# Attention of an audio tower: padded projection weights, folded scale, softmax row sums from a ones column

## The reference, cut to what matters

```python
q = jnp.einsum('bqd,hdm->bqhm', x, W_Q) + b_Q          # k and v alike
scores = jnp.einsum('bqhm,bkhm->bhqk', q, k) / jnp.sqrt(jnp.asarray(D_HEAD, q.dtype))
scores = jnp.where(causal[None, None, :, :], scores, jnp.asarray(IGNORE, scores.dtype))
pattern = jax.nn.softmax(scores, axis=-1)
z = jnp.einsum('bhqk,bkhm->bqhm', pattern, v)
attn_out = jnp.einsum('bqhm,hmd->bqd', z, W_O) + b_O
```

## Time and profile before

| | us |
|---|---|
| median of 3 runs | 1911.6 (1901.9 to 1912.4) |
| span of the profiled execution | 1912.2 |
| PE busy | 1539.1 |
| VectorE busy | 1109.6 |
| ScalarE busy | 757.7 |
| GpSimd busy | 600.9 |

### The profile page before, as it was taken

How to read it: one execution, slowest core, us unless ns; L and a number is a source line. 1 busy time by engine, 2 the same in 40 slices (tenths; PEclk the granted TensorE clock), 3 DMA queues, 4 the chain that set the end, 5 groups by cost and what they waited for, 6 DMA issues and landing times.

```text
span 1912.2 us, 33119 instructions
## 1 busy us (share of the span) xinstructions
PE 1539.1 (80%) x10013; PEld 1020.7 (53%) x10014; DVE 1109.6 (58%) x2520; ACT 757.7 (40%) x1456; POOL 600.9 (31%) x502
## 2 busy tenths in 40 slices
PE   6975699998865899889657999898659999339997
PEld 4332476783333666763334666833336667327775
DVE  5986455568884555669864555598845555302221
ACT  2643344425542444425533444165324443002221
POOL 3732133305431333236322333064213331421111
PEclk6987799998986999979877999989869999659999
DMA  4200121210000221110001222100014332621110
GB/s 125 80 1 1 34 57 41 56 34 12 1 1 1 65 56 41 33 36 1 1 1 40 53 48 51 30 11 1 1 28 105 89 73 66 199 69 46 48 47 20
DMA packets 105852, 81.31 MB, mean 43 GB/s; under 512 B 57842, under 2 KB 96267, under 8 KB 105747
## 3 DMA queue, kind: packets, MB, share of 16 engines
q1 hardware_dynamic: 99988, 70.65, 14.6%
q0 software_dynamic: 5760, 9.36, 1.6%
HBM read 34.66 MB, written 18.38 MB: 28 GB/s over the span
## 4 chain that ended last, share of the span: by engine, by line
issue 40%; PE 35%; POOL 15%; DVE 5%; SPq 2%; DMA 2%; ACT 1%; POOLq 0%; DVEq 0%; ACTq 0%
POOL arena L794 10%; PE ps L1676 8%; PE ps L1618 6%; PE ps L1650 4%; PE ps L1662 3%; PE ps L1830 3%; PE ps L1625 2%; PE ps L1810 2%; PE ps L1811 2%; DVE arena L1212 2%; DVE smax L1203 2%; POOL slot_scratch L848 1%; PE ps L1818 1%; SPq L552 1%; PE ps L1831 1%
## 5 line engine op out<-in xcount | busy, mean ns | idle before, releaser
L1723 PE MATMUL ps<-arena,cwt 128*128 128x504 f16 (+2 forms) x1776 | 409.8, 392 | 85.3 <-DVE arena L1178 59.9
L1723 PEld LDWEIGHTS ps<-arena,cwt 128*128 128x128 f16 x1776 | 179.4, 105 | 305.9 <-DVE arena L1178 66.2
L794 POOL TENSOR_TENSOR arena<-arena 128x1008 f16<-128x1008 f32 (+2 forms) x112 | 255.6, 2292 | 196.6 <-DVE arena L1178 196.6
L1676 PE MATMUL ps<-arena 128*128 128x64 f32 (+2 forms) x2016 | 261.2, 270 | 22.9 <-DVE arena L1212 22.9
L1203 DVE TENSOR_REDUCE smax<-ps 128x1 f32<-128x128 f32 (+5 forms) x288 | 177.2, 615 | 172.1 <-PE ps L1653 172.1
L1676 PEld LDWEIGHTS ps<-arena 128*128 128x128 f32 (+2 forms) x2016 | 242.3, 189 | 44.2 <-issue 28.5
L1212 DVE COPY arena<-ps 128x512 f32<-128x512 f32 (+4 forms) x288 | 157.4, 546 | 83.7 <-PE ps L1662 83.6
L1181 DVE TENSOR_TENSOR arena<-arena 128x1008 f16<-128x1008 f32 (+2 forms) x88 | 200.3, 2276 | 3.0
L917 ACT ACTIVATE arena<-ps,nmax 128x128 f32<-128x128 f32 (+5 forms) x288 | 180.6, 627 | 53.5 <-DVE nmax L1204 50.7
L1178 DVE CAST arena<-arena 128x1008 f16<-128x1008 f32 (+4 forms) x200 | 176.9, 914 | 32.6 <-ACT arena L903 16.1
L1650 PE MATMUL ps<-arena 128*128 128x512 f16 (+6 forms) x780 | 163.7, 313 | 28.9 <-ACT arena L957 16.3
(11 more groups left out here) (249 smaller groups left out, 2181.1 us busy)
## 6 DMA issues: line engine op xcount, KB each, us to landing
arena<-arena SPq DMA_DIRECT2D x96, 187.5 KB, 2.9
arena<-arena SPq DMA_DIRECT2D x96, 93.8 KB, 2.5
slot_scratch<-empty_slot SPq DMA_DIRECT2D x1, 5775.0 KB, 18.6
arena<-in_L_ffn_w SPq DMA_DIRECT2D x8, 576.0 KB
arena<-in_L_ffn_w SPq DMA_DIRECT2D x8, 384.0 KB
arena<-slot_scratch SPq DMA_DIRECT2D x31, 96.5 KB, 1.9
arena<-slot_scratch SPq DMA_DIRECT2D x31, 96.0 KB, 2.0
xa<-in_x POOLq DMA_DIRECT2D x5, 468.8 KB, 4.2
```

Of the source, the lines that this page charges most:

```text
L794: g.tensor_tensor(low, src, high, ALU.subtract).then_inc(S["lo_pool"], 1)
L1676: last = t.matmul(slot(g)[0:m, Z_AT:Z_AT + DH], probt[k % 2][0:kk, c, 0:m], vt[0:kk, c, DH * hh:DH * hh + DH], start=c == 0, stop=c == i)
L1723: last = t.matmul(bank(g, k)[:, 0:c * PITCH].rearrange("p (r c) -> p r c", c=PITCH), cwt[layer][:, w, tap, :], parts[x][:, f:f + 2 * c - 1 ...
```

## The change

The fifth projection term gets 128 rows: `w1_low` is 128 rows high, with zeros set once in rows 64 to 127, against all of `x_rest`. The factor 1/8 moves from the exponential into q and, once at the start, into q's bias; the mask constant shrinks with it. The row max is negated inside the reduce, so L1204 and its semaphore are gone. The exponential has no scale and no accumulator. V's tile gets a 65th column of ones per head (set once per sample in TOWER), so the z matmul of 65 columns leaves the row sum in PSUM beside z. The reciprocal moves from the job pt(k) to the job z(k): VectorE waits for PE's z(k), takes the reciprocal of that column, and ScalarE's drain of z waits for it. VectorE is a reader of z's slot now, after the copy of pt(k+1) in its order.

```diff
-            jobs.append(("z", (k - 1,), (ACT_ENGINE,)))
+            jobs.append(("z", (k - 1,), (DVE_ENGINE, ACT_ENGINE)))
...
-        w1_low = sb("w1_low", [D1, 3, 128], fp16)
+        w1_low = sb("w1_low", [128, 3, 128], fp16)
...
-        vt = take(TT * 128).rearrange("p (t c) -> p t c", c=128)
+        vt = take(TT * 2 * (DH + 1)).rearrange("p (t h c) -> p t h c", h=2, c=DH + 1)
...
                     a.activation(prob[k % PROBS][0:m, 0:128 * i + m], slot(g)[0:m, 0:128 * i + m], ACT.Exp,
-                                 bias=nmax[0:m, k_:k_ + 1], scale=SCALE, accum_out=rsum[0:m, k_:k_ + 1]
-                                 ).then_inc(S["act_freed"], 1)
+                                 bias=nmax[0:m, k_:k_ + 1]).then_inc(S["act_freed"], 1)
...
+                    unscale = (SCALE if kind == "q" else 1.0) / WSCALE
...
-                    wait(act, "rinv_ready", phase, k + 1, b, pr)
+                    wait(act, "dve_freed", phase, freed(phase, DVE_ENGINE, n), b, pr)
...
+            v.memset(w1_low[D1:128, :, :], 0.0).then_inc(pads_ready, 1)
...
-                    step(v.reduce_max(smax[0:m, k_:k_ + 1], slot(g)[0:m, 0:128 * i + m], AX.X))
-                    v.tensor_scalar(nmax[0:m, k_:k_ + 1], smax[0:m, k_:k_ + 1], -SCALE, None, ALU.mult
-                                    ).then_inc(S["smax_done"], 1)
+                    v.reduce_max(nmax[0:m, k_:k_ + 1], slot(g)[0:m, 0:128 * i + m], AX.X, negate=True
+                                 ).then_inc(S["smax_done"], 1)
...
-                    wait(dve, "act_freed", phase, exp_done(phase, k), b, pr)
-                    v.reciprocal(rinv[0:m, k:k + 1], rsum[0:m, k:k + 1]).then_inc(S["rinv_ready"], 1)
+                elif kind == "z":
+                    (k,) = args
+                    m = tile_rows(TILE_ORDER[k % TT])
+                    v.reciprocal(rinv[0:m, k:k + 1], slot(g)[0:m, Z_AT + DH:Z_AT + DH + 1]
+                                 ).then_inc(S["dve_freed"], 1)
...
+            v.tensor_scalar(bqkv[:, 0, :], bqkv[:, 0, :], SCALE, None, ALU.mult).then_inc(q_bias_scaled, 1)
...
+                        if kind == "q":
+                            v.memset(vt[:, :, :, DH:DH + 1], 1.0)
...
-                        (w1_low[:, w, :], xt_parts[0:D1, 2, cols])]
+                        (w1_low[:, w, :], x_rest)]
...
-                        last = t.matmul(slot(g)[0:m, Z_AT:Z_AT + DH], probt[k % 2][0:kk, c, 0:m],
-                                        vt[0:kk, c, DH * hh:DH * hh + DH], start=c == 0, stop=c == i)
+                        last = t.matmul(slot(g)[0:m, Z_AT:Z_AT + DH + 1], probt[k % 2][0:kk, c, 0:m],
+                                        vt[0:kk, c, hh, :], start=c == 0, stop=c == i)
```

More of the change, by code:

```diff
@@ L49 @@
 SCALE = DH ** -0.5
-MASKED = -8.0e5
+MASKED = -1.0e5
 ACT_ENGINE, DVE_ENGINE = "act", "dve"
@@ L112, in pair_jobs @@
         if k:
-            jobs.append(("z", (k - 1,), (ACT_ENGINE,)))
+            jobs.append(("z", (k - 1,), (DVE_ENGINE, ACT_ENGINE)))
     if not last:
         jobs.append(("s", (STEPS + 1,), (ACT_ENGINE,)))
-    jobs.append(("z", (STEPS - 1,), (ACT_ENGINE,)))
+    jobs.append(("z", (STEPS - 1,), (DVE_ENGINE, ACT_ENGINE)))
     if not last:
@@ L226 @@
     "smax_done": (0, 2, STEPS, STEPS - 2, 0),
-    "rinv_ready": (0, 0, STEPS, STEPS, 0),
     "h1_ready": (0, 0, 0, 0, 1),
     "scratch_stored": (16, 0, 0, 0, 64),
-    "dve_step": (14, 35, STEPS, STEPS - 2, 16),
+    "dve_step": (14, 33, 0, 0, 16),
 }
@@ L382, in audio_tower @@
         neg_half = sb("neg_half", [128, TT])
-        smax = sb("smax", [128, STEPS])
         nmax = sb("nmax", [128, STEPS])
-        rsum = sb("rsum", [128, STEPS])
         rinv = sb("rinv", [128, STEPS])
@@ L507, in audio_tower @@
         cw0_stacked = sem("cw0_stacked")
+        q_bias_scaled = sem("q_bias_scaled")
         experts_loaded = sem("experts_loaded")
@@ L763, in split_weights @@
                 g.tensor_tensor(w0_parts[:, 1, :, :], wqkv0[:, :, :], w0_parts[:, 0, :, :], ALU.subtract)
-                g.tensor_tensor(w1_low[:, :, :], wqkv1[0:D1, :, :], w1_high[0:D1, :, :], ALU.subtract
+                g.tensor_tensor(w1_low[0:D1, :, :], wqkv1[0:D1, :, :], w1_high[0:D1, :, :], ALU.subtract
                                 ).then_inc(S["w_split"], 1)
@@ L929, in attention_job @@
                     full = q_full if kind == "q" else k_full
+                    unscale = (SCALE if kind == "q" else 1.0) / WSCALE
                     if phase == TOWER:
                         a.activation(dst[:, 0, :].rearrange("p (k n) -> p k n", k=2), src, ACT.Identity, bias=bias,
-                                     scale=1.0 / WSCALE)
+                                     scale=unscale)
                     a.activation(full.rearrange("p (k n) -> p k n", k=2), src, ACT.Identity, bias=bias,
-                                 scale=1.0 / WSCALE).then_inc(S["act_freed"], 1)
+                                 scale=unscale).then_inc(S["act_freed"], 1)
                 elif kind == "v":
-                    src = slot(g).rearrange("p (t c) -> p t c", c=128)
-                    a.activation(vt[:, 0:TT, :], src[:, 0:TT, :], ACT.Copy, scale=1.0 / WSCALE
+                    src = slot(g)[:, 0:TT * 128].rearrange("p (t h c) -> p t h c", h=2, c=DH)
+                    a.activation(vt[:, :, :, 0:DH], src, ACT.Copy, scale=1.0 / WSCALE
                                  ).then_inc(S["act_freed"], 1)
@@ L960, in _ @@
             act.wait_ge(params_loaded, 16 * n_dmas[params_loaded])
+            act.wait_ge(q_bias_scaled, 1)
             with act.Fori(0, BATCH) as b:
@@ L1063, in _ @@
             v.memset(lnmv[:, :, :], 0.0).then_inc(pads_ready, 1)
-            dve.wait_ge(pads_ready, 6)
+            v.memset(w1_low[D1:128, :, :], 0.0).then_inc(pads_ready, 1)
+            dve.wait_ge(pads_ready, 7)
             dve.wait_ge(weights_loaded, 16 * n_dmas[weights_loaded])
```

## The result

| | before | changed |
|---|---|---|
| median of 4 runs, us | 1910.2 (1901.9 to 1912.4) | 1958.8 (1947.2 to 1973.1) |
| ratio, 95% interval | | 1.027 (1.021 to 1.033) |
| span of the profiled execution | 1912.2 | 1962.5 |

The change makes the kernel 2.7% slower. The forecast was 1900 us with a range of 1876 to 1926, so it is wrong in sign, and the time lies outside the range.

The account below looks back on a forecast made before the run. PE was taken to bound the attention, 727 us or 38% of the span. Padding saves 43 us and the late reciprocal adds 31: 12 less than 1912.2, so 1900 us, range 1876 to 1926.

Parts of the forecast that it names:

- Part 1: Projections q, k, v: padding the 64-row term to 128 rows saves 1.95 us a pair, 43 us in all.
- the first stage: Each sample's first projections, at the lower clock: padding saves 1.0 us, v's 1.2 us hidden behind the head-stacking DMA.
- rival (d): Projections: the padding does nothing, only the late reciprocal's added time remains, 1943 us; chance 0.07.
- Part 2: Row max on VectorE: negating inside the reduce frees 0.21 us a step, 60 us of busy and wait, as cover.
- part 4: z and its drain: row sum as 65th column, reciprocal after z; each hand-over 0.18 us dearer, 30.8 us added.
- z's 65th column: z matmuls on PE: one column more costs 0, as the weight load sets the pace; otherwise 4 us in all.
- Part 3: ScalarE's exponential without sum read-out: 0.1 us of ScalarE a step, at most 0.1 a pair for PE.
- Part 4's walk: Replay of one pair's instructions with the late reciprocal: 1.24 us added a middle pair, 1.49 the last.
- 0.05 from ScalarE to PE: Replay's assumed delay from the end of ScalarE's drain to PE's next load, 0.05 us, read off the old trace.
- (c): PE to z's drain: hand-over dearer, decisive from 0.16 us more at each of eight a pair, 1931 us; chance 0.13.
- marks set for steps: Trace signs: "issue" idle gone, z drain 0.2 us after z, PE's drain waits about 4, middle pair near 31.0.

Follow-up runs that it names:

- e1: The kernel before with only the fifth projection term's weights padded from 64 to 128 rows; 1873.6 us, ratio 0.981.
- e4: The kernel before with padded weights, negated row max and 1/8 folded into q; accumulator and early reciprocal kept; 1855.6 us, ratio 0.971.
- e3: The changed kernel with PE's wait on VectorE left out for slots that z read last, ScalarE's drain implying it; 1901.0 us, ratio 0.994.
- e5: The changed kernel with PE waiting for VectorE before ScalarE instead of after, no wait removed; 1899.5 us, ratio 0.995.
- e6: The changed kernel with six extra, overwritten score matmuls in each of steps 4 and 10 outside TOWER; 1925.7 us, ratio 1.009.
- e8: The kernel before with only the reciprocal moved behind z, and PE's wait on VectorE left out where ScalarE's drain implies it; 1977.5 us, ratio 1.037.

## Why the prediction was wrong

The runs form a ladder that takes the change apart. The attentions of the profiled executions, all four samples, beside the medians:

| | attention, us | step | median | step |
|---|---|---|---|---|
| before | 782.6 | | 1909.9 | |
| e1, padding | 738.2 | -44.4 | 1873.6 | -36.3 |
| e4, and row max, 1/8 | 726.1 | -12.1 | 1855.6 | -18.0 |
| e3, and the late reciprocal from PSUM, one wait | 767.3 | +41.2 | 1901.0 | +45.4 |
| changed, waits in a row | 834.3 | +67.0 | 1958.8 | +57.8 |

The rest of the program varies by up to 7 us from one profiled execution to another (1127.4 in e4, 1134.4 in e3), which is most of the difference between the two columns of steps.

**Part 1, the padding, was right.** Forecast 43 us, found 44.4 in the attention and 36.3 in the medians. The terms now start evenly, 0.16 us apart in q, and in v a group begins 0.28 us after the one before, where the earlier trace rows have 0.48. Timeline of PE in the changed kernel:

```profile
270.59 0.65 PE L1622 MATMUL ps<-arena,w_parts 128*128 128x375 f16 x3 [0.18 <-ACT arena L955]
...
271.08 0.32 PE L1622 MATMUL ps<-arena,w_high 128*128 128x375 f16 x1
...
271.24 0.32 PE L1622 MATMUL ps<-arena,w_low 128*128 128x375 f16 x1
...
271.39 0.64 PE L1622 MATMUL ps<-arena,w_parts 128*128 128x375 f16 x3
...
289.02 0.33 PE L1629 MATMUL ps<-w_parts,arena 128*128 128x128 f16 x3
...
289.30 0.33 PE L1629 MATMUL ps<-w_parts,arena 128*128 128x128 f16 x3
```

Five terms of q take 0.80 us against 1.01 in the earlier trace rows. Two sizes inside it were off and cancel: a pair saves 2.13 us (means of the sixteen middle pairs, 31.66 and 29.53), not 1.95, and the first stage 0.4, not 1.0. The first parts of e1 average 43.08 us against 45.62; take one pair's 2.13 from the 2.54 and 0.4 remain. In the sum the clock rises at the same term as before, behind the fifteenth. In the traces it rises after about the same time behind q's first term, 4.9 to 5.6 us in the four samples before and 4.4 to 5.8 in e1's. By then the closed-up stream has begun 15 to 19 terms instead of 14 to 16, so more of them run at the lower clock, and v begins 0.7 us earlier behind q's first term (5.70 against 6.40, means of four), not 1.0. The other 0.3 are lost between there and the first zt; why is open. In sample 0 of the changed kernel, where q starts at 209.56, the first term at full clock is the last of the twenty of q and k, 5.9 us behind the first:

```profile
214.23 1.15 PE L1622 MATMUL ps<-arena,w_parts 128*128 128x375 f16 x3
215.17 0.45 PE L1622 MATMUL ps<-arena,w_high 128*128 128x375 f16 x1
215.46 0.32 PE L1622 MATMUL ps<-arena,w_low 128*128 128x375 f16 x1
```

The Trainium skill, "TensorEngine Tiling (Array Packing)", Key Properties, on draining at a change of mode: by that rule the gaps on both sides of the 64-row term go, and the trace agrees (0.16 us between all starts). The Trainium skill, "TensorE: Matmul & The Clock Gate", Step-by-step, says that the row count doesn't matter to a load's time. The trace of before agrees for the load itself (0.093 us with 64 rows, 0.098 with 128, medians). I had taken rival (d) to follow from it. It doesn't: the 64-row term costs time by when its load starts, not by how long it takes, and e1, which differs from before in nothing else, is 36 us faster.

**Part 2, row max, was undersized.** I called it cover for part 4 and gave it no gain of its own. Alone it brings 0.5 us in a middle pair and 0.97 in the last, 12 us in the attention and 18 in the medians, since z's wait for VectorE's copy falls from 22.9 us to 5.0. The negation is free: the reduce of 750 columns takes 0.94 us as in the earlier trace rows.

**z's 65th column was right.** Ten weight loads of z take 1.19 us as in the earlier trace rows, and the reciprocal from PSUM 0.165 us where 0.15 was taken. Part 3, the accumulator, has no run of its own: ScalarE has its 288 reads less (1168 instructions against 1456), but what that is worth to PE, 0.1 us a pair at most by the forecast, is not shown.

**Part 4's walk was right as far as it went.** It gave a middle pair of 31.0 and a last one of 24.9, an addition of 30.8 us with part 2's cover in it. e3 and e5 have 30.6 and 24.7, and from e1 to e3 the attention grows by 29.1 us. e5, whose only difference from the change is the order of two waits, takes 1899.5 us, where 1900 was forecast. That it meets it so closely is luck: the forecast took 12 us from 1912.2, while e5 is 8.7 us below the kernel before that was run beside it, and 16.2 below in the attention (766.4 against 782.6).

**The step that failed** is the "0.05 from ScalarE to PE", read off the rows of before and carried over to a kernel in which that hand-over is another. In the earlier trace rows one wait stands in front of the load. The diff makes VectorE a reader of z's slot, so the code that I had named (`slot_free`) issues a second wait there, behind ScalarE's, and that splits two waits on ScalarE that had been one. I had asked what is late on VectorE and ScalarE, and never what PE itself does between the last signal and its load. It is 0.07 to 0.09 us for each wait that stands behind the last to come: 1.07 us in a middle pair, 1.22 in the last, 0.5 in a first part. By the windows of e3 and the changed kernel that makes 16 x 1.07 + 4 x 1.22 + 4 x 0.5 = 24 us; e6 against e3 says 24.7.

**The step that was missing** is the clock. The sum took it at 1.00 in all pairs because it was 1.00 in all pairs before. The changed kernel in sample 1, by stretches of 5 us from the end of one pair into the next:

```profile
670.00:675.00 5.00, 3.76 (x33) 3.20 (x33) 2.19 (x7) 2.73 (x6) 0.71 (x1) 1.00 0.17 39
675.00:680.00 5.00, 4.65 (x38) 3.52 (x37) 2.30 (x5) 1.46 (x3) 0.03 (x1) 1.00 0.18 39
680.00:685.00 5.00, 3.64 (x25) 2.52 (x25) 0.92 (x4) 2.56 (x5) 4.01 (x3) 1.00 0.00 0
685.00:690.00 5.00, 3.57 (x30) 2.80 (x28) 2.95 (x7) 1.94 (x5) 1.95 (x2) 0.99 0.28 65
690.00:695.00 5.00, 5.00 (x29) 5.00 (x29) 1.82 (x5) 1.45 (x4) 0.00 (x0) 0.50 0.68 165
695.00:700.00 5.00, 5.00 (x26) 4.44 (x25) 2.07 (x5) 0.89 (x3) 0.00 (x0) 0.50 0.00 0
700.00:705.00 5.00, 5.00 (x46) 4.80 (x44) 0.76 (x2) 1.81 (x3) 1.60 (x3) 0.65 0.00 0
```

The clock falls at 689.9. PE is busy 3.64 and 3.57 us of the last two times 5 before the clock goes from 2.4 to 1.2 GHz, and then runs without a gap at half speed for over 10 us; this pair is 6.0 us longer than one at full clock. The same two stretches of a pair of sample 0 (305.26 to 315.26) have PE busy 3.63 and 3.57 us, and there the clock stays at 1.00: the same instructions with the same waits do not always bring it down. Such stretches are 43.3 us of the attention. In e6, with two of the waits filled by useless matmuls, they are gone from all twenty pairs. That the filler keeps the clock because PE is busier is the simplest reading, but it also shifts the pair's events against each other, and no run separates the two.

24 and 43 are the 67 us between e3 and the changed kernel. They hang together: e3 and e5 get rid of both at once.

**The rivals.** (c), a dearer hand-over, is the one that happened: 0.13 us at each of eight (1.07/8), where it was to decide from 0.16, and by itself it gives e6's 1925.7. I had put its cause in two semaphores between PE's end and ScalarE's start, and those cost what was forecast; the dear ones are on PE. It had 0.13 of the chances, and none of the rivals had the clock. Of the marks set for steps, the shift of ScalarE's drain by 0.2 us came as described, and the "issue" idle of the projections' loads fell from 1.6 us to 0.4 a pair. The waits of the weight loads for that drain came out at 4.9 + 1.6 = 6.5 us where about 4 was the mark; this and the pair's 31.69 against 31.0 pointed straight at the failed step.

**What stays open.** Which waits bring the clock down was not settled. e3 has waits of PE up to 1.0 us and never loses it; the changed kernel, with 1.2, does in eight of the twenty pairs behind the first ones. e8, which has one wait in front of each load but the 64-row terms and the longer row max, also has PE waits of 1.2 us and loses it in ten of its twenty. Over all runs the longest wait of PE in these pairs is 0.4 to 1.0 us in the six kernels that keep the clock and 1.2 to 1.4 in the four that lose it. But no run changed that wait alone, and within one kernel pairs with the same waits come with and without low clock. How often it falls could not have been worked out from the profile of before.

## What to carry to other kernels

When a change gives a buffer a second reader, count the waits in front of the instruction that reuses it, and put the one that comes last at the end: here two waits swapped are 59 us of 1959. Take a reciprocal or a sum early, beside other work, and keep it off the chain from PE to the drain to PE's next slot: e4 does so and is 5.3% faster than the changed kernel. A 64-row term among 128-row terms is worth padding with zeros. And where a change lengthens PE's waits, look at the clock of every pair, not of one: the stretch that was compared first showed 31.69 us on both sides.

## What was unexpected of the hardware

- A wait that is already fulfilled isn't free when it stands behind one that isn't: 0.07 to 0.09 us each on PE (records at 267.96, 268.06, 268.13), and nothing that can be seen when it stands in front (e5).
- Waits of 0.7 to 1.2 us in a pair of 31.7 are followed by stretches of 10 to 14 us at half clock in pairs whose instructions are the same, and 12 further matmuls a pair make the program 33 us faster (1958.8 to 1925.7).
- Drawing work together in a low-clock stage gained less than the gaps removed, 0.4 us of 1.0: the clock rose 4.9 to 5.6 us behind q's first term with the gaps and 4.4 to 5.8 without, and by then 15 to 19 terms had begun instead of 14 to 16.
